# Keeping x on chip: layer 0's output takes the place of x, and the mask tiles 2 and 3 lose their own buffers

## The chip, the cores and the metric

One core of one Trainium2 chip runs the kernel. The metric is the device time of one execution in microseconds; lower is better.

## The reference, cut to what matters

Two graph attention layers over 8192 nodes with 128 features; each is preceded by a layer norm and a ReLU and added to its input. `adj` is an 8192 x 8192 matrix of int32, about one entry in a thousand of it set.

```python
h = jnp.maximum(_layernorm(x, axis=-1), 0.0)
x = x + _L0_gnn_ref(h, adj, Ws, Wt, Wc)     # softmax(where(adj > 0, (h Ws)(h Wt)^T, -9e15)) @ (h Wc)
h = jnp.maximum(_layernorm(x, axis=-1), 0.0)
x = x + _L1_gnn_ref(h, adj, W, a)           # elu(softmax(masked leaky_relu(s1 + s2)) @ (h W))
```

## The kernel before, in words

The 8192 rows are 64 tiles of 128. SBUF is mostly one tensor, `arena`, cut into regions by word offsets, and almost all data of the large stages lies in it.

**First preparation.** `load_rows` on SyncE's queue brings all of x (4 MB, four DMAs) into `x_all[0]`, a region at `VS` that later stages overwrite. 16 groups of four tiles are normalised (ScalarE and GpSimd, `make_h`), transposed and projected (TensorE), and split into high and low parts (ScalarE, VectorE). GpSimd also issues the loads of the adjacency (`load_chunk`, line 589): a tile is four chunks, each a DMA from int32 in HBM to fp8 in SBUF. In the first preparation it issues the four chunks of tile 0 and then one chunk after each of twelve groups: tiles 1, 2 and 3. Tiles 2 and 3 have buffers of their own (`MASK_AT[2:4]`) in the upper half of `y_rows`, the region at `ADJ` which will hold layer 0's output.

**The tile sweep (layer 0).** `tile_sweep` runs a software pipeline: step i works on tile i (`indicate`: which keys have an edge, a maximum over the mask, VectorE, line 1459), i-1 (`make_pick`, a selection matrix; `pick_mask`, TensorE, line 749, reads the mask), i-2 (`pick_keys` 722, `pick_values` 734, `scores` 761 and 766), i-3 (maximum and exponentials) and i-4 (`weigh`, line 787, and `finish`, which adds x and writes `y_rows`). Six steps are written out, then a loop body of two steps is repeated, then the last steps are written out. A mask chunk may be loaded once `mg_done` says that `pick_mask` is through with the tile that held its buffer: tile 4 waits for tile 0, tile 5 for tile 1, and tile t from 6 on for tile t-2. SyncE's queue stores each tile's selection (`sel_pick`, line 443) and picked mask (`sel`, line 437) to HBM, stores the tile's y to `x_mid` (line 431) and loads x of a later tile into `x_t` (line 426).

**Second preparation and layer 1.** `y_rows` is `x_all[1]`, from which layer 1's inputs are made. Then `batch_sweep`, 64 steps written out in 8 batches of 8, reads `sel_pick` and `sel` back, picks rows (`pick_rows`, TensorE, line 858) and weighs them (`weigh_rows`, line 884). At the seventh step of each batch SyncE's queue loads 8 tiles of `x_mid` into `x8` (line 490) and stores the result of the batch before to `out` (line 492). `above_zero` (line 1741) adds x8.

In the order in which engines run, VectorE, TensorE and ScalarE have fixed, hand-written sequences and wait on semaphores. TensorE's code arrives in the trace as DMA packets of a queue of its own, `q8 instruction`, 16 KB each.

Of the kernel before, what the change touches and what calls it, by code (L numbers as in the profile page):

```python
# [47 lines left out]
def gnn_kernel(nc, x, xB, adj, adjB, Ws, Wt, Wc, W1, a1, out, x_mid, sel, sel_pick):  # L48
# [12 lines left out]
    with ExitStack() as ctx:  # L61
# [22 lines left out]
        cq_lo = part(QQ + 4096, 4096, F16)  # L84
        MASK_AT = (MASK, MASK + 2048, ADJ + 4096, ADJ + 6144)
        mask_8 = [part(at, 2048, F8).rearrange("p (b n) -> p b n", n=P) for at in MASK_AT]
# [32 lines left out]
        W1A = VS + 2 * SB * XW  # L119
        w_raw = [part(at, 2048).rearrange("p (s n) -> p s n", n=P) for at in (W1A, 5120)]  # L120
        w_msk = part(W1A + 2048, 4096).rearrange("p (r s n) -> p r s n", r=2, n=P)
        assert W1A + 6144 <= TOP + 2304 and 5120 + 2048 <= VALS
        m_in = part(MASK + 2048, 1024, F16).rearrange("p (r n) -> p r n", r=2)
        m_in8 = part(MASK + 2048, 1024, F8).rearrange("p (r s n) -> p r s n", r=2, n=P)
        tot = part(0, STEPS * VW).rearrange("p (n v) -> p n v", v=VW)
        x8 = part(2048, STEPS * D).rearrange("p (n d) -> p n d", d=D)
        y8 = part(3072, STEPS * D).rearrange("p (n d) -> p n d", d=D)
        e8 = part(4096, STEPS * D).rearrange("p (n d) -> p n d", d=D)

# [13 lines left out]

        x_all = [part(at, N).rearrange("p (t d) -> p t d", d=D) for at in (VS, ADJ, N, N)]
        X_LOADS = (1, None, 2, 3)
        h_sb = [part(at, 2 * GW).rearrange("p (b n) -> p b n", b=2) for at in (TOP, TOP, 0, 0)]
        hT_sb = [part(at + 2 * GW, 2 * GW).rearrange("p (b n) -> p b n", b=2) for at in (TOP, TOP, 0, 0)]
        a_reps = [None, ca_rep, None, ga_rep]
        x_midB = x_mid.rearrange("(p t) d -> p t d", p=P)

# [107 lines left out]
        adj_in = [[sem(f"adj_in{b}_{c}") for c in range(4)] for b in range(2)]  # L258
        adj_early = [[sem(f"adj_early{b}_{c}") for c in range(4)] for b in range(2)]
        evac_settled = sem("evac_settled")  # L260
# [23 lines left out]
        y_ready = sem("y_ready")  # L284
        x_in = [sem(f"x_in{b}") for b in range(2)]
        y_out = [sem(f"y_out{b}") for b in range(2)]

# [15 lines left out]
        h8_exp = sem("h8_exp")  # L303
        x8_in = sem("x8_in")
        elu_part = sem("elu_part")
# [49 lines left out]
        def there(i, d):  # L355

            return within(i, d, TILES + d)
# [51 lines left out]
        def _(sp):  # L409
# [14 lines left out]

            def load_x(t, b):
                sp.dma_start(x_t[:, b, :], x[bass.ts(t, P), :]).then_inc(x_in[b], 16)

            def store_y(t, b):

                sp.wait_ge(y_ready, t + 1)  # L430
                sp.dma_start(x_midB[:, bass.ds(t, 1), :].rearrange("p o d -> p (o d)"),
                             y_rows[:, bass.ds(t, 1), :].rearrange("p o d -> p (o d)")).then_inc(y_out[b], 16)

            def store_mask(t, b):
# [11 lines left out]
            def tile_io(i, b):  # L446
                if there(i, 1):
                    store_pick(i - 1, 1 - b)
                if there(i, 2):
                    store_mask(i - 2, b)  # L450
                if there(i, 4):
                    store_y(i - 4, b)
                if within(i, 4, TILES + 2):
                    load_x(i - 2, b)
                if isinstance(i, int) and i == 4:
                    sp.wait_ge(mean_ready, 1)
                    sp.dma_start(w_sb[:, 0, :], W1).then_inc(w_in, 16)
# [3 lines left out]
            load_rows(xB, 0, (1, 2, 3))  # L461
            load_x(0, 0)
            load_x(1, 1)
            tile_sweep(sp, tile_io, fetched=False)
            sp.wait_ge(y_out[0], 16 * (TILES // 2))
            sp.wait_ge(y_out[1], 16 * (TILES // 2))
            sp.wait_ge(m_out[0], 16 * (TILES // 2))
# [16 lines left out]
            def selected_keys():  # L484
                def batch_io(j, u):
                    if j or u >= 2:
                        load_selection(j * STEPS + u, u % 2)
                    if u == 6:
                        wait(sp, y8_ready, j)
                        sp.dma_start(x8[:, :, :], x_midB[:, bass.ts(j, STEPS), :]).then_inc(x8_in, 16)  # L490
                        if not isinstance(j, int) or j:
                            sp.dma_start(out[bass.ts(j - 1, CW), :].rearrange("(n p) d -> p n d", p=P), y8[:, :, :]
                                         ).then_inc(y8_out, 16)

                def last_store():
                    for k in range(2):
                        at = slice(k * HALF, k * HALF + HALF)
                        rows = slice((STEPS - 1) * CW + k * HALF * P, (STEPS - 1) * CW + (k + 1) * HALF * P)
                        sp.wait_ge(y8_ready, STEPS + k)
                        sp.dma_start(out[rows, :].rearrange("(n p) d -> p n d", p=P), y8[:, at, :]  # L500
                                     ).then_inc(y8_out, 16)
                    sp.wait_ge(y8_out, 16 * (STEPS + 1))

                batch_sweep(batch_io, last_store)
# [48 lines left out]
        def _(pool):  # L553
# [29 lines left out]
            def load_chunk(t, c):  # L583

                if t >= 4:
                    last = t - 2 if t >= 6 else t - 4
                    pool.wait_ge(mg_done, last * 4 + (c + 1))
                landed = adj_early if 2 <= t < 4 else adj_in
                pool.dma_start(mask_8[t if t < 4 else t % 2][:, c * QCH:(c + 1) * QCH, :], adjB[t, c, :, :, :]  # L589
                               ).then_inc(landed[t % 2][c], 16)  # L590

# [3 lines left out]
            for G in range(PREP):  # L595
                make_h(G, G % 2, 0)
                if G < 12:
                    load_chunk(1 + G // 4, G % 4)
            for t in range(4, TILES):
                for c in range(4):  # L600
                    load_chunk(t, c)
# [26 lines left out]
        def _(pe):  # L628
# [110 lines left out]
            def pick_mask(t, b, q):  # L739

                if q == 0:
                    pe.wait_ge(pick_ready, t + 1)
                wait(pe, m_evac, t * 4 + q)
                settle()
                mask = mask_8[t if isinstance(t, int) and t < 4 else b]
                for s in range(4):
                    for j in range(QB):
                        k = (q * 4 + s) * QB + j
                        last = nc.tensor.matmul(mg_ps[j * SLOT:(j + 1) * SLOT, s * P:(s + 1) * P],  # L749
                                                pick[:, b, k, :], mask[:, k, :],  # L750
                                                start=True, stop=True, skip_group_check=True)
                last.then_inc(mg_done, 1)
# [550 lines left out]
        def _(dve):  # L1303
# [146 lines left out]
            def indicate(t, b, h):  # L1450

                for c in (2 * h, 2 * h + 1):
                    if isinstance(t, int) and t < 4:
                        dve.wait_ge((adj_in if t < 2 else adj_early)[b][c], 16)
                    else:
                        dve.wait_ge(adj_in[b][c], (t - b) * 8)
                at = slice(2 * h * QCH, (2 * h + 2) * QCH)
                mask = mask_u[t if isinstance(t, int) and t < 4 else b]
                nc.vector.reduce_max(ind_raw[:, at], mask[:, at, :], AX_X).then_inc(ind_max, 1)  # L1459
                if h == 1:  # L1460
                    dve.wait_ge(ind_max, t * 2 + 2)
                    nc.vector.tensor_scalar(ind[:, :], ind_raw, 0.0, None, ALU.is_gt).then_inc(ind_ready, 1)
# [49 lines left out]
            def finish(t, b):  # L1512

                dve.wait_ge(inv_done, t + 1)
                dve.wait_ge(x_in[b], (t - b) * 8 + 16)
                own = y_rows[:, bass.ds(t, 1), :].rearrange("p o d -> p (o d)")
                nc.vector.scalar_tensor_tensor(own, pv_ps[:, 0:D], invs[:, bass.ds(t, 1)], x_t[:, b, :],
                                               ALU.mult, ALU.add).then_inc(y_ready, 1)
# [216 lines left out]
            def above_zero(j):  # L1735
# [3 lines left out]
                dve.wait_ge(h8_ready, j + 1)  # L1739
                dve.wait_ge(x8_in, batch * 16 + 16)  # L1740
                nc.vector.scalar_tensor_tensor(x8[:, at, :], y8[:, at, :], 0.0, x8[:, at, :], ALU.max, ALU.add
                                               ).then_inc(elu_part, 1)
# [7 lines left out]
            def finish_b(j):  # L1750

                at = slice(*BATCHES[j][1:])
                dve.wait_ge(elu_part, j * 2 + 2)
                nc.vector.tensor_tensor(y8[:, at, :], x8[:, at, :], e8[:, at, :], ALU.add).then_inc(y8_ready, 1)

# [220 lines left out]
```

## Time and profile before

| | |
|---|---|
| median of 3 runs | 1365.22 us (1362.23 to 1365.72) |
| profiled execution, its own time | 1368.26 us |
| span of the profiled execution | 1366.5 us |
| mean granted TensorE clock | 0.983 |
| TensorE matmul busy | 1273.9 us, 93% |
| VectorE, ScalarE, GpSimd busy | 76%, 72%, 12% |
| adjacency DMA (q0), share of 16 engines over the span | 52.4% |
| other DMA (q1) | 20.2% |

Busy times are shares of the span. The stages by time: the first preparation to about 74 us, the tile sweep to about 905 us, the second preparation to about 949 us, layer 1 to the end.

### The profile page before, as it was taken

How to read it: one execution, taken by the hardware profiler on the slowest of the kernel's cores; microseconds unless marked ns; L12 is line 12 of the kernel's file. 1: busy time of each engine (PE TensorE's matmuls, PEld its weight loads, DVE VectorE, ACT ScalarE, POOL GpSimd, SP SyncE). 2: the span in 40 equal slices, each digit the busy share in tenths (PEclk: the TensorE clock that was granted, in tenths of full speed). 3: DMA queues.
4: the chain of work that ended last, by engine and by line, in shares of the span. 5: the costliest groups of instructions: out<-in, count | busy, mean ns of one | idle time of the engine just before them, and what ended most of it. 6: DMA issues, size and time to landing. Idle time of an engine off the chain costs nothing.

```text
span 1366.5 us, 75053 instructions
## 1 busy us (share of the span) xinstructions
PE 1273.9 (93%) x31691; PEld 1127.8 (83%) x31691; DVE 1044.2 (76%) x2196; ACT 984.7 (72%) x2100; POOL 165.8 (12%) x331
## 2 busy tenths in 40 slices
PE   4868899999999999999999999988999999899996
PEld 3657788888888888888888888876899999899996
DVE  6846467777776777677777767657999999989997
ACT  4855466666676666666666766676899998889995
POOL 4210111111111111111111111021000000000000
PEclk9979899999999999999999999999999999999999
DMA  9673799999999999999999999510334424324432
GB/s 188 77 94 62 93 129 134 140 141 126 141 138 137 128 139 142 128 136 141 139 126 138 141 133 134 103 41 4 99 90 119 123 84 127 111 80 125 113 95 74
DMA packets 103506, 157.58 MB, mean 115 GB/s; under 512 B 11456, under 2 KB 36288, under 8 KB 102848
## 3 DMA queue, kind: packets, MB, share of 16 engines
q0 software_dynamic: 36864, 67.13, 52.4%
q1 hardware_dynamic: 66496, 88.37, 20.2%
q8 instruction: 108, 1.77, 0.5%
q14 instruction: 38, 0.31, 0.1%
HBM read 314.84 MB, written 41.94 MB: 261 GB/s over the span
## 4 chain that ended last, share of the span: by engine, by line
PE 77%; issue 9%; ACT 8%; DVE 4%; DMA 1%; POOL 0%; ACTq 0%; SPq 0%; DVEq 0%; POOLq 0%
PE ps L884 17%; PE ps L787 16%; PE ps L734 11%; PE ps L858 9%; PE ps L766 6%; PE ps L749 4%; PE ps L761 4%; PE ps L722 4%; ACT arena L1118 3%; ACT arena L1127 3%; PE ps L775 1%; PE ps L663 1%; PE ps L881 1%; PE ps L665 1%; PE ps L639 1%
## 5 line engine op out<-in xcount | busy, mean ns | idle before, releaser
L787 PE MATMUL ps<-arena 128*128 128x129 f32 x2048 | 245.6, 278 | 0.0
L884 PE MATMUL ps<-arena 128*128 128x129 f32 x2048 | 244.5, 278 | 0.9 <-issue 0.9
L1134 ACT ACTIVATE arena<-ps,neg_max 128x1024 f32<-128x1024 f32 x128 | 142.3, 1112 | 133.5 <-PE ps L787 133.5
L884 PEld LDWEIGHTS ps<-arena 128*128 128x128 f32 x2048 | 236.1, 193 | 1.1 <-issue 1.1
L787 PEld LDWEIGHTS ps<-arena 128*128 128x128 f32 x2048 | 236.8, 193 | 0.0
L1487 DVE TENSOR_REDUCE mx<-ps 128x1 f32<-128x1024 f32 x128 | 156.8, 1225 | 99.2 <-PE ps L766 98.5
L1118 ACT ACTIVATE arena<-ps 128x512 f32<-128x512 f32 x256 | 152.7, 596 | 99.7 <-PE ps L734 99.7
L589 POOL DMA_DIRECT2D arena<-in_adjB x256 | 136.6, 534 | 687.3 <-PE ps L749 671.7
L1692 DVE TENSOR_SCALAR arena<-arena 128x128 f32<-128x128 f32 x768 | 203.3, 357 | 19.5 <-issue 11.3
L1112 ACT ACTIVATE arena<-ps 128x512 f16<-128x512 f32 x256 | 153.7, 600 | 42.5 <-PE ps L722 40.1
L734 PE MATMUL ps<-arena 128*32 128x128 f16 x8192 | 164.4, 222 | 17.4 <-issue 7.8
L858 PE MATMUL ps<-arena 128*32 128x132 f16 x8192 | 152.7, 225 | 15.0 <-ACT arena L1172 5.4
L1172 ACT ACTIVATE arena<-ps 128x396 f32<-128x396 f32 (+1 forms) x384 | 148.3, 463 | 20.2 <-PE ps L858 20.1
L1127 ACT ACTIVATE arena<-ps 128x512 fp8e4<-128x512 f32 x256 | 152.9, 597 | 12.0 <-PE ps L749 8.9
L766 PEld LDWEIGHTS ps<-arena 128*128 128x128 f16 x2048 | 135.4, 98 | 31.6 <-issue 0.8
L1478 DVE TENSOR_TENSOR arena<-arena 128x2048 fp8e4<-128x2048 f16 x64 | 146.7, 2292 | 17.5 <-DVE arena L1469 17.3
L766 PE MATMUL ps<-arena 128*128 (+1 forms) x2048 | 158.5, 220 | 0.0
L858 PEld LDWEIGHTS ps<-arena 128*32 128x32 fp8e4 x8192 | 130.2, 97 | 33.6 <-issue 17.3
L1459 DVE TENSOR_REDUCE arena<-arena 128x32 f32<-128x1024 uint32 x128 | 154.9, 1210 | 0.0
L1701 DVE SCALAR_TENSOR_TENSOR arena<-arena 128x1024 f32<-128x1024 fp8e4 x128 | 152.3, 1240 | 1.2 <-PE ps L884 0.6
L734 PEld LDWEIGHTS ps<-arena 128*32 128x32 fp8e4 x8192 | 121.5, 97 | 38.4 <-issue 22.6
L722 PE MATMUL ps<-arena 128*128 128x32 fp8e4 x4096 | 143.9, 177 | 2.7 <-issue 2.7
(164 smaller groups left out, 1320.1 us busy)
## 6 DMA issues: line engine op xcount, KB each, us to landing
arena<-in_adjB POOLq DMA_DIRECT2D x256, 256.0 KB, 8.0
sel_pick<-arena SPq DMA_DIRECT2D x64, 256.0 KB, 6.2
sel<-arena SPq DMA_DIRECT2D x64, 256.0 KB, 6.2
arena<-sel_pick SPq DMA_DIRECT2D x64, 256.0 KB, 3.8
arena<-sel SPq DMA_DIRECT2D x64, 256.0 KB, 2.8
arena<-in_xB SPq DMA_DIRECT2D x4, 1024.0 KB, 6.0
x_t<-in_x SPq DMA_DIRECT2D x64, 64.0 KB, 4.9
x_mid<-arena SPq DMA_DIRECT2D x64, 64.0 KB, 5.1
```

Source lines behind the costliest of these rows:

```text
L722: last = nc.tensor.matmul(kg_ps[:, k * SLOT:(k + 1) * SLOT], kp[:, g * SB + k, :], pick[:, b, g * SB + k, :], start=True, stop=True)
L734: last = nc.tensor.matmul(vg_ps[j * SLOT:(j + 1) * SLOT, s * D:(s + 1) * D], pick[:, b, k, :], c_vals[:, k, l * D:(l + 1) * D], start=(l = ...
L766: last = nc.tensor.matmul(dst[:, k * P:(k + 1) * P], k_sel[:, at:at + P], rows[:, bass.ts(t, P)], start=False, stop=(n == 1), skip_group_c ...
L787: last = nc.tensor.matmul(pv_ps, p_T[:, s * P:(s + 1) * P], v_sel[:, b, s, :], start=False, stop=(s == SB - 1), skip_group_check=True)
L858: last = nc.tensor.matmul(xg_ps[g % 3][j * SLOT:(j + 1) * SLOT, at:at + XW], pick[:, b, s * QB + j, :], wv[:, s * QB + j, l, :], start=(l ...
L884: last = nc.tensor.matmul(xv_ps[b], w_msk[:, b, s, :], x1_sel[:, b, s, 0:VW], start=False, stop=(s == SB - 1), skip_group_check=True)
L1112: nc.scalar.activation(k_sel[:, g * GW:(g + 1) * GW], kg_ps, ACT.Copy).then_inc(k_evac, 1)
L1118: nc.scalar.activation(v_sel[:, b, 4 * g:4 * g + 4, 0:D], vg_ps.rearrange("p (s v) -> p s v", v=D), ACT.Copy).then_inc(v_evac, 1)
L1127: nc.scalar.activation(m_sel8[:, b, 4 * q:4 * q + 4, :].rearrange("p s n -> p (s n)"), mg_ps, ACT.Copy, bias=-1.0, saturate=False).then_in ...
L1459: nc.vector.reduce_max(ind_raw[:, at], mask[:, at, :], AX_X).then_inc(ind_max, 1)
L1487: nc.vector.reduce_max(mx[:, h:h + 1], ps[:, 2 * h:2 * h + 2, :].rearrange("p b n -> p (b n)"), AX_X).then_inc(part_max, 1)
L1692: last = nc.vector.tensor_scalar(w_raw[b][:, k, :], own, x1_sel[:, b, k, D + 2:D + 3], x1_sel[:, b, k, D + 1:D + 2], ALU.mult, ALU.max)
```

## The change

x is loaded once, into the region at `ADJ`, and stays there. `finish` adds `pv / denominator` to the row of x in place, so the tile of output replaces its tile of x. The loads of x by tile, the stores of y to `x_mid` and the reloads of `x_mid` into `x8` are gone (64, 64 and 8 DMAs). As the upper half of `ADJ` is now occupied, tiles 2 and 3 use the two ordinary mask buffers and wait for tiles 0 and 1. Small buffers of layer 1 that lay in the region move elsewhere.

```diff
-        MASK_AT = (MASK, MASK + 2048, ADJ + 4096, ADJ + 6144)
+        MASK_AT = (MASK, MASK + 2048)
...
-        w_raw = [part(at, 2048).rearrange("p (s n) -> p s n", n=P) for at in (W1A, 5120)]
+        w_raw = [part(at, 2048).rearrange("p (s n) -> p s n", n=P) for at in (W1A, VALS + NB * XW)]
...
-        tot = part(0, STEPS * VW).rearrange("p (n v) -> p n v", v=VW)
-        x8 = part(2048, STEPS * D).rearrange("p (n d) -> p n d", d=D)
-        y8 = part(3072, STEPS * D).rearrange("p (n d) -> p n d", d=D)
-        e8 = part(4096, STEPS * D).rearrange("p (n d) -> p n d", d=D)
+        tot = part(POSX + NB, STEPS * VW).rearrange("p (n v) -> p n v", v=VW)
+        y8 = part(CC + 1024, STEPS * D).rearrange("p (n d) -> p n d", d=D)
+        e8 = part(E8, STEPS * D).rearrange("p (n d) -> p n d", d=D)
...
-        x_all = [part(at, N).rearrange("p (t d) -> p t d", d=D) for at in (VS, ADJ, N, N)]
+        x_all = [part(at, N).rearrange("p (t d) -> p t d", d=D) for at in (ADJ, ADJ, N, N)]
...
-                if there(i, 4):
-                    store_y(i - 4, b)
-                if within(i, 4, TILES + 2):
-                    load_x(i - 2, b)
...
-            load_x(0, 0)
-            load_x(1, 1)
             tile_sweep(sp, tile_io, fetched=False)
-            sp.wait_ge(y_out[0], 16 * (TILES // 2))
-            sp.wait_ge(y_out[1], 16 * (TILES // 2))
+            sp.wait_ge(vg_done, TILES * 4)
...
-                    if u == 6:
-                        wait(sp, y8_ready, j)
-                        sp.dma_start(x8[:, :, :], x_midB[:, bass.ts(j, STEPS), :]).then_inc(x8_in, 16)
-                        if not isinstance(j, int) or j:
-                            sp.dma_start(out[bass.ts(j - 1, CW), :].rearrange("(n p) d -> p n d", p=P), y8[:, :, :]
-                                         ).then_inc(y8_out, 16)
+                    if u == 6 and j:
+                        sp.wait_ge(y8_ready, j)
+                        sp.dma_start(out[bass.ts(j - 1, CW), :].rearrange("(n p) d -> p n d", p=P), y8[:, :, :]
+                                     ).then_inc(y8_out, 16)
...
-                if t >= 4:
-                    last = t - 2 if t >= 6 else t - 4
-                    pool.wait_ge(mg_done, last * 4 + (c + 1))
-                landed = adj_early if 2 <= t < 4 else adj_in
-                pool.dma_start(mask_8[t if t < 4 else t % 2][:, c * QCH:(c + 1) * QCH, :], adjB[t, c, :, :, :]
-                               ).then_inc(landed[t % 2][c], 16)
+                if t >= 2:
+                    pool.wait_ge(mg_done, (t - 2) * 4 + (c + 1))
+                pool.dma_start(mask_8[t % 2][:, c * QCH:(c + 1) * QCH, :], adjB[t, c, :, :, :]
+                               ).then_inc(adj_in[t % 2][c], 16)
...
-                if G < 12:
-                    load_chunk(1 + G // 4, G % 4)
-            for t in range(4, TILES):
+                if G < 4:
+                    load_chunk(1, G)
+            for t in range(2, TILES):
...
-                dve.wait_ge(x_in[b], (t - b) * 8 + 16)
                 own = y_rows[:, bass.ds(t, 1), :].rearrange("p o d -> p (o d)")
-                nc.vector.scalar_tensor_tensor(own, pv_ps[:, 0:D], invs[:, bass.ds(t, 1)], x_t[:, b, :],
+                nc.vector.scalar_tensor_tensor(own, pv_ps[:, 0:D], invs[:, bass.ds(t, 1)], own,
...
-                dve.wait_ge(x8_in, batch * 16 + 16)
-                nc.vector.scalar_tensor_tensor(x8[:, at, :], y8[:, at, :], 0.0, x8[:, at, :], ALU.max, ALU.add
+                rows = y_rows[:, batch * STEPS + lo:batch * STEPS + hi, :]
+                nc.vector.scalar_tensor_tensor(rows, y8[:, at, :], 0.0, rows, ALU.max, ALU.add
```

The orders of TensorE's, ScalarE's and VectorE's computing instructions are the same in both kernels. GpSimd's queue differs at the end of the first preparation (578 is `make_h`, 589 `load_chunk`; in the changed kernel these are lines 555 and 564). Before, from the group that begins x's last quarter on:

```order
L589 DMA arena<-in_adjB 128x2048
L578 TENSOR_SCALAR arena<-arena,rstd 128x128 [waits hT_ps_ready,xall_in3,rstd_ready]
L578 TENSOR_SCALAR arena<-arena,rstd 128x128
L578 TENSOR_SCALAR arena<-arena,rstd 128x128 [waits hT_ps_ready,xall_in3,rstd_ready]
L578 TENSOR_SCALAR arena<-arena,rstd 128x128
L589 DMA arena<-in_adjB 128x2048 [waits mg_done] x240
```

In the changed kernel, after the last chunk of tile 1, which follows the fourth group:

```order
L564 DMA arena<-in_adjB 128x2048
L555 TENSOR_SCALAR arena<-arena,rstd 128x128 [waits hT_ps_ready,xall_in1,rstd_ready]
L555 TENSOR_SCALAR arena<-arena,rstd 128x128
L555 TENSOR_SCALAR arena<-arena,rstd 128x128 [waits hT_ps_ready,xall_in3,rstd_ready]
L555 TENSOR_SCALAR arena<-arena,rstd 128x128
L564 DMA arena<-in_adjB 128x2048 [waits mg_done] x248
```

Eight chunks have moved from between the groups to behind all of them, and 248 instead of 240 chunks wait for `mg_done`.

SyncE's queue in layer 1, at the seventh step of a batch; before:

```order
L475 DMA arena<-sel_pick 128x1024 [waits xg_done]
L478 DMA arena<-sel 128x1024 [waits w_ready]
L490 DMA arena<-x_mid 128x1024 [waits y8_ready]
L492 DMA out_x<-arena 128x8x128
L475 DMA arena<-sel_pick 128x1024 [waits xg_done]
L478 DMA arena<-sel 128x1024 [waits w_ready]
```

In the changed kernel:

```order
L454 DMA arena<-sel_pick 128x1024 [waits xg_done]
L457 DMA arena<-sel 128x1024 [waits w_ready]
L469 DMA out_x<-arena 128x8x128 [waits y8_ready]
L454 DMA arena<-sel_pick 128x1024 [waits xg_done]
L457 DMA arena<-sel 128x1024 [waits w_ready]
```

The load from `x_mid` ahead of the store is gone, and the store carries its wait.

## Rows read from the trace of the kernel before

**Rows 1.** The page's first line, the whole execution.

```profile
span 1366.5 us, 75053 instructions
```

**Rows 2.** Busy by stretch: length; PE, PEld, DVE, ACT, POOL; PEclk, DMA share, GB/s.

```profile
99.15:111.62 12.47, 11.03 (x296) 9.48 (x289) 8.06 (x12) 6.31 (x12) 0.00 (x0) 0.93 0.16 49
111.62:124.71 13.09, 12.24 (x329) 10.64 (x328) 9.07 (x15) 8.44 (x15) 0.00 (x0) 1.00 0.17 58
124.71:143.10 18.39, 13.54 (x324) 11.63 (x323) 9.15 (x15) 8.12 (x15) 2.12 (x4) 0.81 0.77 95
143.10:161.09 17.99, 13.46 (x324) 11.79 (x323) 9.00 (x14) 8.32 (x14) 2.12 (x4) 0.85 0.78 97
161.09:175.90 14.81, 14.53 (x342) 12.84 (x341) 8.99 (x14) 9.38 (x15) 2.12 (x4) 0.95 0.71 97
400.00:600.00 200.00, 195.38 (x5230) 172.03 (x5229) 143.44 (x225) 135.15 (x224) 33.93 (x64) 1.00 1.04 136
```

**Rows 3.** TensorE's timeline, 56 to 160 us, rows of interest.

```profile
108.44 0.29 PE L734 MATMUL ps<-arena 128*32 128x128 f16 x6 [1.37 <-issue]
...
119.86 0.52 PE L734 MATMUL ps<-arena 128*32 128x128 f16 x23 [0.64 <-issue]
...
121.94 3.79 PE L787 MATMUL ps<-arena 128*128 128x129 f32 x32
...
137.80 0.29 PE L749 MATMUL ps<-arena 128*32 128x128 fp8e4 x1 [4.33 <-issue]
...
157.34 0.59 PE L734 MATMUL ps<-arena 128*32 128x128 f16 x13 [4.24 <-issue]
...
158.00 5.93 PE L787 MATMUL ps<-arena 128*128 128x129 f32 x32
```

**Rows 4.** DMA queues, 129 to 160 us: packets, MB, share of 16 engines.

```profile
q0 software_dynamic: 1144, 2.09, 77.0%
...
q8 instruction: 4, 0.07, 0.8%
```

**Rows 5.** DMA queues, 102 to 127 us; the view lists no q0.

```profile
q8 instruction: 4, 0.07, 1.1%
```

**Rows 6.** DMA queues, 400 to 600 us.

```profile
q0 software_dynamic: 9172, 16.71, 89.2%
```

**Rows 7.** GpSimd's timeline: the second and fourth chunk issued for tile 4.

```profile
76.46 0.53 POOL L589 DMA_DIRECT2D arena<-in_adjB  x1 [0.91 <-PE ps L749]
...
79.40 0.53 POOL L589 DMA_DIRECT2D arena<-in_adjB  x1 [0.97 <-PE ps L749]
```

**Rows 8.** Line 589: landing of those two chunks, in this order.

```profile
DMA to landing us min/median/max: 9.4/9.4/9.4
...
DMA to landing us min/median/max: 11.3/11.3/11.3
```

**Rows 9.** VectorE's timeline, 84 to 94 us.

```profile
84.51 1.21 DVE L1459 TENSOR_REDUCE arena<-arena 128x32 f32<-128x1024 uint32 x1
89.13 1.23 DVE L1487 TENSOR_REDUCE mx<-ps 128x1 f32<-128x1024 f32 x1 [3.41 <-PE ps L766]
...
90.60 1.21 DVE L1459 TENSOR_REDUCE arena<-arena 128x32 f32<-128x1024 uint32 x1
...
93.84 0.29 DVE L1500 TENSOR_REDUCE arena<-ps 128x1 f32<-128x128 f32 x1 [1.80 <-PE ps L775]
```

**Rows 10.** TensorE's timeline in layer 1, rows of interest.

```profile
1183.57 3.79 PE L884 MATMUL ps<-arena 128*128 128x129 f32 x32
...
1192.36 0.30 PE L858 MATMUL ps<-arena 128*32 128x132 f16 x8 [2.90 <-issue]
...
1192.66 5.43 PE L884 MATMUL ps<-arena 128*128 128x129 f32 x32
...
1344.17 2.61 PE L884 MATMUL ps<-arena 128*128 128x129 f32 x21 [0.87 <-issue]
```

**Rows 11.** DMA queues, 1184 to 1191 us.

```profile
q1 hardware_dynamic: 1522, 1.68, 87.7%
```

More of the change, by code:

```diff
@@ L119, in gnn_kernel @@
         W1A = VS + 2 * SB * XW
-        w_raw = [part(at, 2048).rearrange("p (s n) -> p s n", n=P) for at in (W1A, 5120)]
+        w_raw = [part(at, 2048).rearrange("p (s n) -> p s n", n=P) for at in (W1A, VALS + NB * XW)]
         w_msk = part(W1A + 2048, 4096).rearrange("p (r s n) -> p r s n", r=2, n=P)
-        assert W1A + 6144 <= TOP + 2304 and 5120 + 2048 <= VALS
+        E8 = VALS + NB * XW + 2048
+        assert W1A + 6144 <= TOP + 2304 and E8 + STEPS * D <= QQ
         m_in = part(MASK + 2048, 1024, F16).rearrange("p (r n) -> p r n", r=2)
         m_in8 = part(MASK + 2048, 1024, F8).rearrange("p (r s n) -> p r s n", r=2, n=P)
-        tot = part(0, STEPS * VW).rearrange("p (n v) -> p n v", v=VW)
-        x8 = part(2048, STEPS * D).rearrange("p (n d) -> p n d", d=D)
-        y8 = part(3072, STEPS * D).rearrange("p (n d) -> p n d", d=D)
-        e8 = part(4096, STEPS * D).rearrange("p (n d) -> p n d", d=D)
+        tot = part(POSX + NB, STEPS * VW).rearrange("p (n v) -> p n v", v=VW)
+        y8 = part(CC + 1024, STEPS * D).rearrange("p (n d) -> p n d", d=D)
+        e8 = part(E8, STEPS * D).rearrange("p (n d) -> p n d", d=D)
         z = part(0, 2 * N).rearrange("p (b n) -> p b n", b=2)
@@ L148, in gnn_kernel @@
         a_reps = [None, ca_rep, None, ga_rep]
-        x_midB = x_mid.rearrange("(p t) d -> p t d", p=P)
         SPANS = [((0, 16), (16, 32), (32, 64)), ((0, 48), (48, 64)), ((0, TILES),), ((0, TILES),)]
@@ L258, in gnn_kernel @@
         adj_in = [[sem(f"adj_in{b}_{c}") for c in range(4)] for b in range(2)]
-        adj_early = [[sem(f"adj_early{b}_{c}") for c in range(4)] for b in range(2)]
         evac_settled = sem("evac_settled")
@@ L284, in gnn_kernel @@
         y_ready = sem("y_ready")
-        x_in = [sem(f"x_in{b}") for b in range(2)]
-        y_out = [sem(f"y_out{b}") for b in range(2)]
         m_ld = [sem(f"m_ld{b}") for b in range(2)]
@@ L303, in gnn_kernel @@
         h8_exp = sem("h8_exp")
-        x8_in = sem("x8_in")
         elu_part = sem("elu_part")
@@ L423, in load_weights @@
                     sp.dma_start(a_sb[:, :], a1.rearrange("(k d) o -> d (k o)", k=2)).then_inc(w_in, 16)
[L425 to L432, printed above, removed]
             def store_mask(t, b):
@@ L744, in pick_mask @@
                 settle()
-                mask = mask_8[t if isinstance(t, int) and t < 4 else b]
+                mask = mask_8[b]
                 for s in range(4):
@@ L1452, in indicate @@
                 for c in (2 * h, 2 * h + 1):
[L1453 to L1456, printed above, removed]
+                    dve.wait_ge(adj_in[b][c], (t - b) * 8 + 16)
                 at = slice(2 * h * QCH, (2 * h + 2) * QCH)
-                mask = mask_u[t if isinstance(t, int) and t < 4 else b]
+                mask = mask_u[b]
                 nc.vector.reduce_max(ind_raw[:, at], mask[:, at, :], AX_X).then_inc(ind_max, 1)
@@ L1750, in finish_b @@
             def finish_b(j):
-                at = slice(*BATCHES[j][1:])
+                batch, lo, hi = BATCHES[j]
+                at = slice(lo, hi)
+                rows = y_rows[:, batch * STEPS + lo:batch * STEPS + hi, :]
                 dve.wait_ge(elu_part, j * 2 + 2)
-                nc.vector.tensor_tensor(y8[:, at, :], x8[:, at, :], e8[:, at, :], ALU.add).then_inc(y8_ready, 1)
+                nc.vector.tensor_tensor(y8[:, at, :], rows, e8[:, at, :], ALU.add).then_inc(y8_ready, 1)
             def selected_keys():
```

## The prediction

> **What bounds the kernel now.** I read the busy times by stretch first. In the steady part of the tile sweep TensorE's matmuls are busy for 195.38 of 200 us at a granted clock of 1.00, that is at 2.4 GHz, while the 16 DMA engines show a share of 1.04 [rows 2]. So two resources look full at once: TensorE and the DMA engines, of which the adjacency loads alone take 89.2% [rows 6]. What matters is which one waits. In the steady sweep no VectorE reduction over the mask has idle time ahead of it that a DMA ends, and the list of waits names no DMA for line 1459 or for line 1517, which reads x. The DMA traffic is large but arrives in time; the period, about 12.5 us a tile, is TensorE's.
>
> The start of the sweep is another matter. I cut it at the moments when SyncE stores a tile's selection, one per step. The steps last 12.47, 13.09, 18.39, 17.99 and 14.81 us [rows 2]. The two of 18 us hold two gaps on TensorE of 4.33 and 4.24 us that the profile puts down to "issue": nothing visible ended them. Each lies in the middle of a run of identical matmuls (one of sixteen, thirteen of thirty-two left over), where the code waits for nothing [rows 3]. The same kind of gap is in the two quick steps, but only 1.37 and 0.64 us long [rows 3]. The reader should compare the DMA queues under them: 129 to 160 us the adjacency queue q0 takes 77.0% and four blocks of TensorE's own code arrive on q8 [rows 4]; 102 to 127 us again four blocks arrive, but q0 is silent [rows 5]. I read the gaps as TensorE waiting for its code, longer where the block queues behind adjacency packets. After a gap the clock drops as well: mean 0.81 and 0.85 in those steps, a mixture of 1.2 and 2.4 GHz [rows 2], and the run of 32 weighing matmuls takes 5.93 us instead of 3.79 [rows 3]. From about the ninth step the loop repeats and no code arrives; the effect belongs to the start alone.
>
> **The change, part by part.**
>
> *x loads and y stores in the sweep (128 DMAs of 64 KB).* Nobody waits for them, TensorE sets the period, and the instruction that adds x keeps its shape. Value 0. From below, if all of TensorE's idle time in the steady part were due to DMA traffic, 4.62 us in 200, over some 700 us of steady sweep, would come back: 16 us [rows 2]. I take 0, since the idle pieces that I looked at are fractions of a microsecond next to ScalarE's evictions, not to DMAs.
>
> *Eight mask chunks that are no longer issued in the first preparation.* Their cover there was idle DMA time; GpSimd's issues are not on the path of the groups, which keep their pace with and without a chunk. Value 0 in the preparation. What is late next is the mask of tile 2. Its chunks are issued at the moments when tile 4's were, since they wait for the same `mg_done`. The second is issued at 76.46 and lands 9.4 us later, at 85.9; the fourth at 79.40, landing 11.3 us later, at 90.7 [rows 7, 8]. VectorE wants the first half at 84.51 and the second at 90.60. So it starts 1.4 and 0.1 us late, but behind these it has idle waits for TensorE of 3.41 and 1.80 us [rows 9]. Both delays are hidden: 0 us. If chunks landed so much later that 3.41 us were used up, each further microsecond would be on the path. Tile 3's chunks, read the same way, have over 4 us to spare.
>
> *The adjacency queue is no longer silent in the fourth and fifth step.* Before, tiles 4 and 5 were loaded while 0 and 1 were being finished, and then nothing could be loaded until tile 4 was through: that is the silence at 102 to 127 us. After the change the loads of tiles 4 and 5 fall there, in the rhythm of the steady sweep. So code blocks that came through a quiet queue now meet a full one, in two steps. Upper bound: both steps become like the two long ones. Excess over 12.5 us: 5.89 and 5.49 for those, -0.03 and 0.59 for the quick ones [rows 2], so 11.38 - 0.56 = +10.8 us. Lower bound: the blocks happen to fall into lulls, 0. Of the long steps' blocks not every one caused a gap, so I stay below the middle of a full repeat plus its clock loss: I take +7 us. This is the largest term and the least certain.
>
> *The eight reloads of `x_mid` in layer 1.* Each batch has a burst on SyncE's queue: x8 load, output store, selections. In the burst at 1184 us the queue moves 1.68 MB in 7 us at 87.7% of the engines [rows 11], 0.24 MB a microsecond; without the reload of 128 x 1024 fp32, 0.52 MB, it is 2.2 us shorter. Layer 1 is written out, so code blocks arrive all the time, and one gap of 2.90 us stands at the end of this burst, followed by weighing matmuls of 5.43 instead of 3.79 us; a second gap of 0.87 us stands behind the last burst [rows 10]. Bounds: 0 (the gap stays) and 2.90 + 1.64 + 0.87 = 5.4 us (all gone). I take -2.5 us, the burst's 2.2 and a little of the clock.
>
> *The rest* costs nothing: the changed end of SyncE's sweep lets the first selections be read sooner, under the second preparation; the in-place sums have the shapes that they had; buffers that moved are read by the same instructions.
>
> **The Trainium skill weighed.** The rows show gaps where code arrives through a busy queue [rows 3 to 5]. The Trainium skill, page "Runtime: NRT & Kernel Launch", section "Instruction fetch mechanics", says that the sequencer fetches the next 16 KB block while the current one executes and that the cost of crossing a block is mostly hidden. By that rule the term of +7 would be 0. The gaps of 4.33 and 4.24 us speak against it here; that the two gaps in the quiet queue are short speaks for it. The skill's page "DMA: Bandwidth & Descriptors", section "Queues, rings and completion order", adds that each DMA engine takes the queues in turn, a whole packet at a time, which would explain a block that arrives late among adjacency packets; no run here shows the turns themselves.
>
> **Sum.** 0 + 0 + 7 - 2.5 = +4.5 us. Against the profiled execution's 1368.26 us (its span is 1366.5 [rows 1], 1.8 less) that is 1372.8. That execution is 3.0 us above the median of the runs, which is what a gap such as the one at 1192 us would add. On the median, 1365.22 + 4.5 = 1369.7 us.
>
> **The rivals.** A: as above, code gaps in the fourth and fifth step, slower by more than 0.3% (about 4.1 us, which is about what a measurement of this kernel can tell from no change); 1369.7 us, chance 0.46.
>
> B: the blocks stay mostly hidden, or the gain in layer 1 evens it out, within 0.3%. For it: gaps depend on where a block meets a lull, and the long steps have lulls too. With +2 instead of +7 the sum is -0.5: 1364.7 us, chance 0.35.
>
> C: faster, by layer 1's bursts. Place: the seventh step of each batch. Price: up to 5.4 us, the gaps of 2.90 and 0.87 us and the longer weighing behind one. It decides if the start of the sweep loses less than 1.3 us, since 5.4 less that is 4.1. Against it: only one of eight bursts had a long gap, and the median run has perhaps none. 1359.8 us, chance 0.12.
>
> D: masks late. It starts to cost when tile 2's second chunk takes over 11.5 us (84.51 + 3.41 - 76.46) to land. If its 9.4 us doubled [rows 8], VectorE would be 10.8 us late, less 3.41 hidden: 7.3 us on top of A, 1377.0 us. Against it: in the changed kernel the queue is emptier at that moment, not fuller. Chance 0.04.
>
> E: the steady period shortens with less DMA traffic, up to 16 us: 1354 us by 1365.22 + 4.5 - 16. Against it: no wait there names a DMA. Chance 0.03.
>
> **How the numbers follow.** Slower is A and D, 0.50; same is B, 0.35; faster is C and E, 0.15. The range reaches down into C and up to the full repeat of two long steps with no gain in layer 1, 1365.22 + 10.8 = 1376.0, plus the spread of the runs: 1361 to 1377.5 us.
>
> **What would show it.** In the profile after, the steady stretch must keep 195.4 of 200 us and the period of 12.5. The steps between the selection stores of tiles 2, 3 and 4 must grow from 12.5 and 13.1 us, with "issue" gaps inside runs of matmuls and a granted clock below 1, while q0 is busy between 102 and 127 us. VectorE's first reduction over tile 2 must show a wait for a DMA of about 1.4 us, and the next maximum must start no later. In layer 1 the bursts must be some 2 us shorter and the gap at their end smaller. I am wrong if the fourth and fifth steps keep their length with q0 busy under them, if the early steps wait for masks, or if the steady period moves.

## The result

Measured side by side, the changed kernel takes 1371.39 us (median of 12 runs, 1366.74 to 1374.50), the kernel before 1366.35 us. The ratio is 1.0041, with a 95% interval of 1.0030 to 1.0052: 5.6 us slower by the ratio (the medians lie 5.0 us apart), clear of noise.

The first line of the page, and of the DMA queues the one that lost traffic (packets, MB, share):

```profile
span 1371.7 us, 74591 instructions
...
q1 hardware_dynamic: 46912, 75.78, 16.9%
```

12.6 MB of traffic are gone (88.37 MB before), and the span is 5.2 us longer than in [rows 1]. Busy time by stretch, cut at the same events as [rows 2] (the selection stores of tiles 2 to 7) and the same steady stretch; columns: stretch, length, PE, PEld, DVE, ACT, POOL, PEclk, DMA share, GB/s:

```profile
100.06:116.52 16.46, 11.28 (x251) 9.41 (x252) 8.17 (x12) 5.54 (x11) 2.11 (x4) 0.71 0.83 99
116.52:134.37 17.85, 15.08 (x330) 13.26 (x329) 9.05 (x15) 8.65 (x14) 2.11 (x4) 0.79 0.76 94
134.37:150.55 16.18, 14.02 (x344) 12.39 (x343) 9.15 (x15) 9.72 (x16) 2.11 (x4) 1.00 0.76 96
150.55:167.01 16.46, 12.48 (x315) 10.82 (x315) 9.00 (x14) 7.35 (x14) 2.11 (x4) 0.83 0.87 103
167.01:181.85 14.84, 14.56 (x342) 12.86 (x341) 8.99 (x14) 9.38 (x15) 2.11 (x4) 0.95 0.68 88
400.00:600.00 200.00, 195.44 (x5230) 172.24 (x5230) 143.47 (x225) 134.77 (x224) 33.39 (x64) 1.00 1.03 126
```

The steady stretch is what it was; its DMA traffic fell from 136 to 126 GB/s and bought nothing. The two steps that took 12.47 and 13.09 us take 16.46 and 17.85 us. The two after them gave something back: 16.18 and 16.46 instead of 18.39 and 17.99 us. TensorE's timeline of those steps, rows of interest (brackets: idle time before, and what ended it):

```profile
107.64 0.57 PE L709 MATMUL ps<-arena 128*32 128x128 f16 x26
113.19 0.40 PE L709 MATMUL ps<-arena 128*32 128x128 f16 x6 [4.99 <-issue]
...
113.66 5.50 PE L762 MATMUL ps<-arena 128*128 128x129 f32 x32
...
128.39 0.83 PE L709 MATMUL ps<-arena 128*32 128x128 f16 x23 [2.56 <-issue]
...
145.94 0.23 PE L724 MATMUL ps<-arena 128*32 128x128 fp8e4 x1 [1.87 <-issue]
...
163.28 0.59 PE L709 MATMUL ps<-arena 128*32 128x128 f16 x13 [3.69 <-issue]
```

The gaps stand at the same matmuls as in [rows 3]: ahead of the last 6, 23, 1 and 13. The first two grew from 1.37 and 0.64 to 4.99 and 2.56 us, and 32 weighing matmuls behind the first take 5.50 us instead of 3.79. The DMA queues from 102 to 127 us, silent on q0 in [rows 5]:

```profile
q0 software_dynamic: 760, 1.39, 64.8%
...
q8 instruction: 3, 0.05, 0.7%
```

The moments at which single code blocks start tie them to the gaps. In the changed kernel, read microsecond by microsecond, q8 has one packet between 101 and 102 us, none from 102 to 110, and the next between 110 and 111:

```profile
q8 instruction: 1, 0.02, 6.3%
```

The gap ends at 113.19. In the kernel before, the corresponding packet starts between 106 and 107 us and the gap ends at 108.44. At the second gap the packet starts between 125 and 126 us, the gap ending at 128.39; before, between 117 and 118, the gap ending at 119.86. So in all four cases TensorE goes on 2 to 3 us after a code block has started to arrive. Not every block brings a gap: blocks that start between 131 and 132 us and between 148 and 149 us, with q0 at 99.0% and 100.3% in those microseconds, have none behind them.

VectorE's timeline where tile 2's mask is first wanted:

```profile
85.83 1.22 DVE L1431 TENSOR_REDUCE arena<-arena 128x32 f32<-128x1024 uint32 x1 [0.47 <-DMA arena<-in_adjB]
89.90 1.22 DVE L1459 TENSOR_REDUCE mx<-ps 128x1 f32<-128x1024 f32 x1 [2.85 <-PE ps L741]
```

It waits 0.47 us for the load and 2.85 us for TensorE right behind. That maximum starts 0.77 us later than in [rows 9], but so did the maximum ahead of the wait (84.14 us, before 83.37), so the later mask added nothing. In layer 1, the gap of 2.90 us in [rows 10] has a smaller twin at the same matmuls:

```profile
1196.91 0.30 PE L833 MATMUL ps<-arena 128*32 128x132 f16 x8 [1.25 <-issue]
...
1197.21 3.79 PE L859 MATMUL ps<-arena 128*128 128x129 f32 x32
```

### The profile page after: what moved, and what is told of

It reads as the page before. It is cut to its first block, busy times and chain, and to the rows that moved or that the text cites. A ratio compares the mean times of both kernels' runs of the same rounds, so it can differ in the third digit from the quotient of the medians.

```text
span 1371.7 us, 74591 instructions
## 1 busy us (share of the span) xinstructions
PE 1277.5 (93%) x31691; PEld 1130.5 (82%) x31691; DVE 1044.0 (76%) x2196; ACT 984.4 (72%) x2100; POOL 165.0 (12%) x331
## 4 chain that ended last, share of the span: by engine, by line
PE 77%; issue 9%; ACT 8%; DVE 4%; DMA 1%; POOL 0%; ACTq 0%; SPq 0%; DVEq 0%; POOLq 0%
PE ps L859 17%; PE ps L762 16%; PE ps L709 10%; PE ps L833 10%; PE ps L741 6%; PE ps L724 4%; PE ps L736 4%; PE ps L697 4%; ACT arena L1093 3%; ACT arena L1102 3%; PE ps L750 1%; PE ps L638 1%; PE ps L856 1%; PE ps L614 1%; PE ps L640 1%
```

## The experiments

"Two steps" below are those between the selection stores of tiles 2, 3 and 4: 25.6 us before, 34.3 us after. They are read in one profiled execution each and scatter: experiment 2, whose sweep is that of the kernel before, shows 26.6 us. A ratio is always to runs of the kernel before on the same chip.

**1. The fetch alone.** The kernel before, with tiles 2 and 3 in the ordinary buffers.

```diff
-        MASK_AT = (MASK, MASK + 2048, ADJ + 4096, ADJ + 6144)
+        MASK_AT = (MASK, MASK + 2048)
...
-                if G < 12:
-                    load_chunk(1 + G // 4, G % 4)
-            for t in range(4, TILES):
+                if G < 4:
+                    load_chunk(1, G)
+            for t in range(2, TILES):
```

> The kernel before with one part of the change alone: tiles 2 and 3 use the two ordinary mask buffers and wait for tiles 0 and 1; the loads of x, the stores of y and the reloads of x_mid all stay. Code theory (TensorE's code blocks queue behind adjacency packets in the fourth and fifth step): this part carries the whole loss. The two steps between the selection stores of tiles 2, 3 and 4, 25.6 us before and 34.3 us in the changed kernel, become 32 to 36 us, q0 is busy between 102 and 127 us, and the time is 4 to 9 us above the kernel before. Rival (the loss lies in the in-place work of either layer): the two steps keep 25.6 us and the time is within 1 us of the kernel before.

Ratio 1.0069 (1.0048 to 1.0091), medians 1373.98 and 1364.62 us. SyncE's queue at the three stores, then TensorE's two gaps between them:

```profile
99.34 0.34 SPq L443 DMA_DIRECT2D sel_pick<-arena  x1
113.99 0.34 SPq L443 DMA_DIRECT2D sel_pick<-arena  x1
129.86 0.35 SPq L443 DMA_DIRECT2D sel_pick<-arena  x1
```

```profile
110.67 0.40 PE L732 MATMUL ps<-arena 128*32 128x128 f16 x6 [2.48 <-issue]
125.01 0.51 PE L732 MATMUL ps<-arena 128*32 128x128 f16 x23 [2.03 <-issue]
```

The two steps take 30.5 us in the profiled execution, below the 32 to 36 I gave, and the time 9.4 us more, at the top of it. The profiled execution itself, 1372.13 us, is 1.9 below its median. The two steps of one execution are thus a rough measure: with q0 busy for 73.2% of 102 to 127 us they are 3.8 us shorter than in the changed kernel. The loss is here and not in the in-place work.

**2. Layer 1's part alone.** The kernel before, with `above_zero` in place and no reload.

```diff
-                        sp.dma_start(x8[:, :, :], x_midB[:, bass.ts(j, STEPS), :]).then_inc(x8_in, 16)
...
-                nc.vector.scalar_tensor_tensor(x8[:, at, :], y8[:, at, :], 0.0, x8[:, at, :], ALU.max, ALU.add
+                nc.vector.scalar_tensor_tensor(rows, y8[:, at, :], 0.0, rows, ALU.max, ALU.add
```

> The kernel before with only layer 1's part of the change: no reload of x_mid, above_zero adds in place, tot, y8, e8 and one half of w_raw in their new places. The sweep is untouched. Burst theory: 1 to 4 us faster than the kernel before, with the bursts at the seventh step of a batch some 2 us shorter. Rival: nobody waits for the reloads and code gaps there come and go by chance, so within 1 us of the kernel before.

Ratio 0.9991 (0.9976 to 1.0006): 1.2 us faster at the centre, 2.35 us between the medians, and not told apart from nothing: the interval runs from 3.3 us faster to 0.8 us slower. The DMA queue in a 7 us window over the burst of the same batch, against 87.7% in [rows 11], and TensorE behind it:

```profile
q1 hardware_dynamic: 1326, 1.05, 48.5%
```

```profile
1189.31 0.30 PE L856 MATMUL ps<-arena 128*32 128x132 f16 x8 [0.88 <-issue]
```

By these windows the burst is (0.877 - 0.485) x 7 = 2.7 us shorter; over 20 us around it (47.4% from 1175 to 1195 us before, 37.3% from 1172 to 1192 here) it is 2.0 us. The gap is 0.88 instead of 2.90 us. It is not the chance of one execution. All five profiled executions with the reload show it at 2.06 to 2.90 us; the smallest is that of experiment 1:

```profile
1196.80 0.30 PE L856 MATMUL ps<-arena 128*32 128x132 f16 x8 [2.06 <-issue]
```

The six without the reload, in which TensorE's code is not moved, show 0.88 to 1.25 us at the same matmuls. The 32 weighing matmuls behind take 5.43 us in three of the five (the kernel before, experiments 7 and 9) and 3.79 us in all six.

**3. Traffic that nothing needs.** The kernel before, with the chunks of tiles 2 and 3 loaded a second time once they are picked. (In the loop VectorE also has a wait for these loads; the profile shows no idle time that it causes.)

```diff
             for t in range(4, TILES):
+                if t == 6:
+                    for s in (2, 3):
+                        for c in range(4):
+                            pool.wait_ge(mg_done, s * 4 + (c + 1))
+                            pool.dma_start(mask_8[s][:, c * QCH:(c + 1) * QCH, :], adjB[s, c, :, :, :]
+                                           ).then_inc(spare_in, 16)
```

> The kernel before plus eight loads that nothing needs: once a chunk of tile 2 or 3 is picked, the same chunk is loaded again into its buffer, so q0 is busy between 102 and 127 us as in the changed kernel, while every mask is there as early as before. Code theory: traffic alone makes the loss; the two steps of 25.6 us become 31 to 36 us, with issue gaps inside runs of matmuls, and the time is 4 to 9 us above the kernel before. Rival (the changed kernel waits for its masks or for a buffer): no mask is later here, so the steps keep 25.6 us and the time stays.

Ratio 1.0056 (1.0034 to 1.0077). TensorE's first gap, then the stores of tiles 2 and 4:

```profile
112.21 0.40 PE L741 MATMUL ps<-arena 128*32 128x128 f16 x6 [5.53 <-issue]
```

```profile
98.81 0.34 SPq L444 DMA_DIRECT2D sel_pick<-arena  x1
...
133.66 0.35 SPq L444 DMA_DIRECT2D sel_pick<-arena  x1
```

34.9 us, as in the changed kernel, with every mask as early as before. (This execution, 1378.40 us, is the slowest of its six; their median is 1373.48.) Traffic alone makes a loss of that size.

**4. The changed kernel with the early fetch back**, in eight chunk buffers: five in gaps of `arena`, one behind the mean rows, two in the space of `u_t`, `x_t` and `y_t`, which this path does not use.

```diff
+        EARLY_AT = [(CC + 1024, CC + 1536, POSX + NB, POSX + NB + 512),
+                    (POSX + NB + 1024, END + 256, None, None)]
...
+                to = early_8(t, c) if 2 <= t < 4 else mask_8[t % 2][:, c * QCH:(c + 1) * QCH, :]
```

> The changed kernel with tiles 2 and 3 fetched in the first preparation again, into eight chunk buffers found in gaps of the SBUF layout (x still stays on chip, no loads of x, no stores of y). Code theory: the two steps go back from 34.3 to about 25.6 us and the time to that of the kernel before less whatever layer 1 gains: 1 to 4 us below the kernel before. Rival (the loss is in the in-place work): still some 5 us above it.

Ratio 0.9998 (0.9985 to 1.0012). The stores of tiles 2 and 4:

```profile
100.69 0.33 SPq L443 DMA_DIRECT2D sel_pick<-arena  x1
...
124.63 0.33 SPq L443 DMA_DIRECT2D sel_pick<-arena  x1
```

23.9 us for the two steps: the loss is gone. The gain of 1 to 4 us did not show; the interval reaches from 2.0 us faster to 1.6 us slower.

**5. The quiet restored by small loads.** The changed kernel; tiles 4 and 5 load one block in sixteen.

```diff
-                pool.dma_start(mask_8[t % 2][:, c * QCH:(c + 1) * QCH, :], adjB[t, c, :, :, :]
+                n = 1 if t in (4, 5) else QCH
+                pool.dma_start(mask_8[t % 2][:, c * QCH:c * QCH + n, :], adjB[t, c, :, 0:n, :]
```

> The changed kernel, but of tiles 4 and 5 each chunk's load brings one block in sixteen; the rest of the buffer keeps the mask of tile 2 or 3, so two tiles of the output are not the reference's. All waits and their order stay. Code theory: q0 is nearly silent between 102 and 127 us as in the kernel before, the two steps between the selection stores of tiles 2, 3 and 4 fall from 34.3 to 25 to 28 us, and the gaps before the last six and the last twenty-three of thirty-two matmuls (4.99 and 2.56 us) shrink to about 1.4 and 0.6 us; the time is 4 to 8 us below the changed kernel's. Rival (waiting for the buffers of tiles 2 and 3 costs): tiles 2 and 3 are loaded as in the changed kernel, so nothing changes.

Ratio 0.9980 (0.9965 to 0.9995). The stores:

```profile
100.90 0.33 SPq L429 DMA_DIRECT2D sel_pick<-arena  x1
112.33 0.33 SPq L429 DMA_DIRECT2D sel_pick<-arena  x1
125.42 0.33 SPq L429 DMA_DIRECT2D sel_pick<-arena  x1
```

24.5 us. Waits and buffers are those of the changed kernel; only the bytes of two tiles are missing, and the loss with them.

**6. The code moved by half a block.** The changed kernel with 128 more TensorE instructions ahead of everything.

```diff
+            for _ in range(128):
+                pe.sem_inc(pe_shift, 1)
```

> The changed kernel with 128 semaphore increments that nobody waits for ahead of TensorE's first instruction, half of a 16 KB block of its code. If the gaps are TensorE waiting for a block of code, each moves by half a block: some 62 matmuls earlier in the sequence than before, so none is left ahead of the last six of thirty-two matmuls of pick_values, and the new places are about 124 matmuls apart. Time: within 5 us of the changed kernel, either way, since the blocks meet other moments of the queue. If the gaps have another cause (a semaphore, a DMA of data), they stay at the same matmuls.

Ratio 1.0052 (1.0036 to 1.0067). TensorE's timeline there:

```profile
109.86 0.61 PE L710 MATMUL ps<-arena 128*32 128x128 f16 x29
113.33 0.24 PE L710 MATMUL ps<-arena 128*32 128x128 f16 x3 [2.86 <-issue]
113.46 0.41 PE L725 MATMUL ps<-arena 128*32 128x128 fp8e4 x16
113.79 0.33 PE L751 MATMUL ps<-ident,arena 128*128 128x128 f32 x1
113.96 0.57 PE L698 MATMUL ps<-arena 128*128 128x32 fp8e4 x16
114.46 1.04 PE L710 MATMUL ps<-arena 128*32 128x128 f16 x32
```

The last row is the run that was broken after 26 of its 32 matmuls; now it is whole. The gap has gone 3 + 16 + 1 + 16 + 26 = 62 matmuls up, the half block that 128 instructions are. The gaps ahead of the last 1 and the last 13 have gone 62 and 61 up as well. The one ahead of the last 23 has none at its place or 62 up, but one 62 further down, where the shifted code has its next boundary. A gap that follows the instruction count and not the data is a gap of code.

**7. Half the dose.** As 3, with tile 3's four spare loads only.

```diff
-                    for s in (2, 3):
+                    for s in (3,):
```

> The kernel before plus four spare loads instead of eight, those of tile 3 alone. The dose: code theory gives about half of what eight cost (8.9 us by medians), 2 to 6 us above the kernel before, and the step after tile 2's selection store stays at 12.5 us while the one after tile 3's grows to 15 to 18 us. Rival (any load there breaks the rhythm for good): as much as eight.

Ratio 1.0014 (0.9998 to 1.0029), medians 2.2 us apart. The stores:

```profile
100.43 0.34 SPq L444 DMA_DIRECT2D sel_pick<-arena  x1
111.81 0.34 SPq L444 DMA_DIRECT2D sel_pick<-arena  x1
127.29 0.35 SPq L444 DMA_DIRECT2D sel_pick<-arena  x1
```

11.4 us without a load beneath, 15.5 us with. The time is at the lower end of the 2 to 6 us forecast, and its interval just includes no change.

**8. Early fetch and moved code** (4 and 6 together; the two edits as shown there).

> The changed kernel with early fetch of tiles 2 and 3 again and the code shifted by 128 instructions, to see if another place of the blocks saves part of the two gaps that stay in the first pass of the loop (2.14 and 3.42 us there). Code theory: the gaps move, the time is between 5 us below and 5 us above the kernel before; no better guess. Rival: same places, same time as without the shift.

Ratio 0.9998 (0.9982 to 1.0013). Moving the boundaries did not help.

**9. Plain copies in place of adjacency loads.** The kernel before, with eight copies of 512 KB from x to `out` on SyncE's queue at the moments of the spare loads.

```diff
+            def spare(n):
+                sp.wait_ge(mg_done, 9 + n)
+                sp.dma_start(out[n * CW:(n + 1) * CW, :], x[n * CW:(n + 1) * CW, :]).then_inc(spare_in, 16)
```

> The kernel before plus eight plain copies of 512 KB from x to the output (overwritten later) on SyncE's own queue, one at each moment at which a spare load of tile 2 or 3 was issued. So the DMA engines are busy between 102 and 127 us with q1's packets, and q0 stays silent. If any traffic on the DMA engines delays TensorE's code blocks, the two steps of 25.6 us grow to 30 us or more and the time rises by 3 to 9 us; if it takes q0's (adjacency) packets, the steps stay within 1.5 us of 25.6 and the time within 2 us. I hold the second at 4 in 10: in layer 1 the blocks also met q1 bursts, mostly without a gap.

Ratio 1.0037 (1.0018 to 1.0056). The queue from 102 to 127 us (no q0 listed), then the stores of tiles 2 and 4:

```profile
q1 hardware_dynamic: 964, 4.75, 57.7%
```

```profile
99.08 0.34 SPq L444 DMA_DIRECT2D sel_pick<-arena  x1
...
128.49 0.35 SPq L444 DMA_DIRECT2D sel_pick<-arena  x1
```

29.4 us, with gaps of 2.11 and 2.29 us at the known matmuls. It need not be the adjacency queue; the outcome that I held at 4 in 10 did not come, though 29.4 falls a little short of the 30 us given for the other. All these experiments add traffic or take it away; none tells a wait for the DMA engines from one for the memory behind them.

**10. At most two chunks in flight**, in the changed kernel, tiles 2 to 9.

```diff
+                if 2 <= t < 10:
+                    was_t, was_c = divmod(t * 4 + c - 2, 4)
+                    pool.wait_ge(adj_in[was_t % 2][was_c], 16 * (was_t // 2 + 1))
```

> The changed kernel, but for tiles 2 to 9 GpSimd issues a chunk only when the chunk two before it has landed, so at most two are in flight. If a code block waits behind everything that q0 has queued on its DMA engine, the gaps shrink to 1 to 2 us and the time falls by 3 to 6 us against the changed kernel (ratio to the kernel before 1.000 to 1.002). If the queues take turns packet by packet, the depth of q0's queue does not matter and the time stays at 1.004, or rises where a mask comes late.

Ratio 1.0054 (1.0035 to 1.0074). GpSimd's timeline shows the limit at work, TensorE's the two gaps:

```profile
80.79 0.53 POOL L567 DMA_DIRECT2D arena<-in_adjB  x1 [3.88 <-DMA arena<-in_adjB]
```

```profile
112.22 0.40 PE L712 MATMUL ps<-arena 128*32 128x128 f16 x6 [3.06 <-issue]
127.89 0.76 PE L712 MATMUL ps<-arena 128*32 128x128 f16 x23 [2.29 <-issue]
```

In the changed kernel up to four chunks were in flight under the first gap (107.4 to 108.5 us) and three under the second. With two, the first gap is 3.06 instead of 4.99 us and the second 2.29 instead of 2.56, but the two steps last 34.1 us and the time did not fall; q0 is busy for 66.9% of 102 to 127 us, against 64.8%. So a shallower queue was no shield here. The Trainium skill, page "DMA: Bandwidth & Descriptors", section "Queues, rings and completion order", says that each DMA engine takes its queues in turn, a packet at a time; by that rule the backlog would not matter, and the time agrees. The size of the delay is another thing: the 760 packets of q0 in the changed kernel took 0.648 x 25 x 16 / 760 = 0.34 us each, and one such packet ahead of a code block is far less than the 3.6 us by which the first gap grew. What the block waits for in that time is not shown, nor whether the page's packet is one of the trace's.

**11. The same limit for tiles 6 to 9, on top of experiment 2.**

```diff
+                if 6 <= t < 10 and t * 4 + c >= 26:
+                    was_t, was_c = divmod(t * 4 + c - 2, 4)
+                    pool.wait_ge(adj_in[was_t % 2][was_c], 16 * (was_t // 2))
```

> The kernel before with layer 1's part of the change, and at most two chunks in flight for tiles 6 to 9, where the two gaps of 4.33 and 4.24 us lie. If the depth of q0's queue matters: 2 to 5 us faster than the layer 1 part alone (ratio to the kernel before 0.995 to 0.998). If not: 0.999 as without it.

Ratio 1.0014 (0.9998 to 1.0030), a miss on both sides: not 0.995 to 0.998, and not 0.999 either, though its interval overlaps that of experiment 2.

No version that I ran beats the kernel before clearly. The one below 1 with its whole interval, experiment 5, leaves work out.

## Why the prediction was right, point by point

**Rival A came about**, slower by 5.6 us where +4.5 was forecast (1369.7 us; the median is 1371.39, beside 1366.35 for the kernel before in the same comparison). The wait, its place and its sign were right. That the sum came so close is in part luck: by their ratios the two parts measured alone give 9.4 - 1.2 = +8.2 us, and the 2.6 us between that and the whole are not explained, though the intervals allow for them.

**The x loads and y stores, 0.** The steady stretch kept its 195.4 of 200 us. Whether they matter at the start of the sweep is open: experiment 1 with its loads and stores stands at 1.0069, the changed kernel at 1.0041, and layer 1's part explains 0.0009 of the difference; the intervals do not settle the rest.

**The late mask of tile 2, hidden.** Forecast 1.4 us late, measured 0.47 us of waiting, with 2.85 us of idle time behind. Experiment 3 confirms it from the other side: all masks early, same loss.

**The fourth and fifth step, +7.** That traffic delays TensorE's code is shown by experiments 1, 3, 5, 6, 7 and 9 and by the moments at which the blocks start. The size was a choice, not a sum: the prediction says that it stays below the middle of a full repeat, but the middle of 0 and 10.8 is 5.4, and 7 lies above it. It was still low for the fetch alone: 9.4 us by medians. Within the profiled execution the two steps cost 34.31 - 25.56 = 8.75 us, nearer the upper bound of 10.8 than I put it; in experiment 1 they cost 5.0, in experiment 3 9.3. I took the next two steps as unchanged. In these two executions they gave 3.7 us back (36.4 before, 32.6 after), but they scatter: 35.0 us in experiment 2 with the sweep of the kernel before, 37.6 in experiment 1 with the fetch of the changed kernel. How much of the 3.7 belongs to the change is not shown.

**Layer 1, -2.5.** Measured 1.2 us by the ratio and 2.35 between medians, an interval that holds both 0 and the forecast, so the runs do not settle the size. The burst did get shorter, by 2.0 to 2.7 us (2.2 forecast). The prediction priced the gap from one execution and doubted that the others had it. They do: with the reload it is 2.06 to 2.90 us in five profiled executions, without it 0.88 to 1.25 in six. The pieces agree with the term: some 1.3 us of gap, and 1.64 us of slow weighing in three of the five.

**The rule that the prediction weighed.** The Trainium skill, page "Runtime: NRT & Kernel Launch", section "Instruction fetch mechanics", says that crossing a 16 KB block is mostly hidden. Where the DMA engines are quiet the traces come near to that: gaps of 1.37 and 0.64 us. With busy engines it is not safe: up to 5.53 us at one block in experiment 3, while other blocks pass with no gap, as at 131 and 148 us in the changed kernel. The loop says nothing on it, as no code arrives there.

## What to carry to other kernels

Straight-line code is DMA traffic: where TensorE ran through code for the first time, its next block shared the DMA engines with the data, and a gap marked "issue" in the middle of a run of like instructions is its trace. Before a prefetch is moved, look at what runs where it lands: here eight loads left a stretch in which they cost nothing for one in which TensorE was taking in code, and the data was in time all the same. Traffic that nobody waited for was worth nothing when it was removed from the steady loop, even at a DMA share of 1.04.

## What the runs showed that I had not expected

- 57.7% of the engines busy with plain copies lengthened the two steps by 3.85 us. Adjacency loads did so by 5.0 us in experiment 1 (73.2%), 8.75 in the changed kernel (64.8%) and 9.3 in experiment 3. Both queues delay code; with such a scatter, one execution of each does not say which delays it more.
- Limiting the loads in flight to two shortened the first gap by 1.9 us, and yet neither the two steps (34.1 us) nor the time.
- Around a gap the clock pays as well: the mean granted clock was 0.71 in the first of the two steps, 0.93 before. As a mixture of 2.4 and 1.2 GHz that is (1 - 0.71) / 0.5 = 58% of the step at the lower level. The gap is not the cause of all of it. The means of short stretches are 0.53 and 0.61 from 100 to 104 us, ahead of the gap; 1.00 from 104 to 110; 0.59 from 110 to 112, inside it; 0.50 from 112 to 116, and 0.70 from 116 to 118. What the lower level costs behind the gap is seen in the weighing matmuls, 5.50 us instead of 3.79.
